# A decoder of four layers on one core: slots of two cross attentions interleaved with the closing steps around them, and a mixture's routing split by batches

## The reference

```python
x = x + L0_xattn(norm(x), ctx, ctx, mask)      # 16 heads of 8, additive mask
x = x + L0_ffn(norm(x))                        # mixture: 8 experts, top 2, one shared, GELU
x = x + L1_attn(norm(x))                       # "hyperbolic": softmax(-arccosh(q.k)^2 / sqrt(8))
x = x + L1_xattn(norm(x), ctx, ctx)            # 16 heads of 8
x = x + L1_ffn(norm(x))                        # mixture: 8 experts, top 2, one shared, SwiGLU

def L0_ffn(x):
    probs = softmax(x @ w_router.T)            # 8 logits for each token
    gates = one_hot_top2(probs) * values
    y = gelu(x @ W1 + b1) @ W2 + b2            # each expert, weighted by its gate
    return SCALE * (shared(x) + sum_e gates_e * y_e)
```

## Time and profile before

| what | us |
|---|---|
| median of 3 runs | 1261.74 (1260.95 to 1270.15) |
| the profiled execution, its own time | 1260.36 |
| its span, first to last instruction | 1259.0 |
| around the span | 1.4 |
| PE busy | 1029.4 (82%) |
| DVE busy | 803.8 (64%) |
| ACT busy | 609.9 (48%) |
| mean granted TensorE clock | 0.867 |

### The profile page before, as it was taken

One profiled execution on the slowest core, in us unless ns is written; L12 is line 12 of the kernel. 1 busy time (PEld: TensorE's weight loads), 2 busy tenths in 40 slices (PEclk: granted clock), 3 DMA queues, 4 the chain that ended last, 5 costly groups with the idle time before them and its releaser, 6 DMA issues.

```text
span 1259.0 us, 19879 instructions
## 1 busy us (share of the span) xinstructions
PE 1029.4 (82%) x7630; PEld 552.7 (44%) x7649; DVE 803.8 (64%) x2003; ACT 609.9 (48%) x1015; POOL 241.3 (19%) x305
## 2 busy tenths in 40 slices
PE   5777689998999974678585889999848978769999
PEld 4233223333577652344352233556513333336757
DVE  7786867722214467977856883487688877765412
ACT  2456345664333527768651778423115645423342
POOL 2923400000000223676441000000122000010000
PEclk9788879998899995757776899899956889989999
DMA  8332140000000210238012400800100300000000
GB/s 299 93 84 71 39 164 2 2 2 1 1 1 1 78 57 1 76 126 144 10 44 77 162 2 3 140 1 1 51 2 25 127 2 2 34 1 1 1 9 9
DMA packets 34785, 61.23 MB, mean 49 GB/s; under 512 B 4771, under 2 KB 25076, under 8 KB 33092
## 3 DMA queue, kind: packets, MB, share of 16 engines
q1 hardware_dynamic: 33828, 58.64, 16.6%
q10 hardware_dynamic: 864, 1.33, 0.3%
HBM read 42.91 MB, written 16.65 MB: 47 GB/s over the span
## 4 chain that ended last, share of the span: by engine, by line
PE 59%; DVE 28%; ACT 5%; issue 4%; DMA 2%; POOL 1%; SPq 0%; DVEq 0%; ACTq 0%; POOLq 0%
PE ps_s L869 9%; PE ps_e L859 9%; PE ps_v L662 6%; PE ps_e L598 5%; DVE mx L1816 5%; PE ps_s L619 3%; PE ps_e L596 3%; DVE ps_s L1812 2%; PE ps_s L943 2%; PE ps_e L956 2%; ACT work L1364 2%; DVE mx L1806 2%; DVE work L2290 2%; DVE work L2292 2%; DVE xn L1772 1%
## 5 line engine op out<-in xcount | busy, mean ns | idle before, releaser
L1364 ACT ACTIVATE work<-ps_e 128x512 f32<-128x512 f32 x448 | 250.8, 598 | 148.2 <-PE ps_e L598 143.0
L2557 POOL TENSOR_TENSOR rstd<-rstd,halves 128x2 f32<-128x2 f32 x52 | 36.6, 705 | 714.0 <-DVE rstd L1759 713.9
L1816 DVE TENSOR_REDUCE mx<-ps_s 128x2 f32<-128x1024 f32 x128 | 153.8, 1221 | 28.6 <-PE ps_s L619 27.1
L619 PE MATMUL ps_s<-ctx_stack,q_stack 49*128 49x512 bf16 (+1 forms) x384 | 130.2, 459 | 45.4 <-DVE mx L1816 32.9
L598 PE MATMUL ps_e<-q_stack,ctx_stack 52*128 52x256 bf16 (+1 forms) x768 | 151.2, 295 | 19.0 <-issue 6.5
L1466 ACT ACTIVATE work<-ps_s,keep 128x512 f32<-128x512 f32 x136 | 93.0, 687 | 144.8 <-PE ps_s L869 141.9
L662 PE MATMUL ps_v<-work,vaug 128*32 128x256 f32 x1536 | 131.9, 420 | 4.6 <-ACT work L1352 4.6
L859 PEld LDWEIGHTS ps_e<-ffn_w,work 128*128 128x128 f32 x960 | 119.1, 198 | 21.1 <-issue 19.9
L869 PE MATMUL ps_s<-xnT,ffn_w 128*128 128x512 f32 x240 | 119.2, 624 | 3.6 <-ACT work L1466 3.6
L859 PE MATMUL ps_e<-ffn_w,work 128*128 128x128 f32 x960 | 120.9, 281 | 0.8 <-DVE x L2006 0.8
L2016 DVE SCALAR_TENSOR_TENSOR x<-ps_e,gates,x 128x128 f32<-128x128 f32 x128 | 38.9, 346 | 126.5 <-PE ps_e L859 123.5
(11 more groups left out here) (375 smaller groups left out, 1800.7 us busy)
## 6 DMA issues: line engine op xcount, KB each, us to landing
q_stack<-q_scr SPq DMA_DIRECT2D x32, 192.0 KB
ffn_w<-in_L0f_w SPq DMA_DIRECT2D x1, 4608.0 KB, 14.7
ffn_w<-in_L1f_w SPq DMA_DIRECT2D x1, 3456.0 KB, 13.1
q_scr<-parts SPq DMA_DIRECT2D x16, 192.0 KB, 2.1
c_scr<-ffn_w SPq DMA_DIRECT2D x12, 256.0 KB, 7.5
kx_scr<-ffn_w SPq DMA_DIRECT2D x12, 256.0 KB, 3.4
ctx_stack<-kx_scr SPq DMA_DIRECT2D x2, 1536.0 KB
ctx_stack<-c_scr SPq DMA_DIRECT2D x2, 1536.0 KB
```

The lines of the kernel that those rows point to most:

```text
L619: return pe.matmul(ps_s[i][:, parity, :], q_stack[p0:p0 + n_rows, b, pair, part * P:(part + 1) * P], ctx_stack[p0:p0 + n_rows, pair, b * S ...
L1364: act.activation(pt[:, parity, :, :].rearrange("p k q -> p (k q)"), bank[f"e{parity}"], ACT.Exp).then_inc(exped, 1)
L1816: m = dve.tensor_reduce(mx[:, b, :, pair, part], ps_s[i][:], AX, ALU.max, negate=True)
```

## The change

1. **X0's end.** The main loop stops before slot 86 (TAILX). `l0_mixture` runs slots 86 to 95 itself with window_tile, and puts the 12 ups and their GELUs before slots 87 to 93 (1, 1, 2, 2, 2, 2, 2). On ACT too, the GELUs of a slot stand before what the slot itself does.
2. **L0 routing in two parts.** Batches 0 and 1 are routed in bank m at slot 66 of X0 (ACT's exponential and DVE's route_rest at slot 67), batches 2 and 3 after slot 95 in ps_s1, with DVE's route_rest at unit 1. The first half's gates and bias stand before unit 0, the second half's before unit 3 (GATES1).
3. **L1 routing.** The first half moves from slot 86 of X1 to slot 66, from bank e0 to m.
4. **X1's slots 16 to 19** go between the closing steps of the L1 attention's last batch: 16 before turn_close, 17 before l1_project_out, 18 before turn_norm, 19 before project. On DVE, slots 16 and 17 stand before add_out, 18 before the normalise, 19 after it.

```diff
+CLOSE_X1 = 4
+TAILX = 86
+GELU_FIRST = [(u, j) for u in range(3) for j in range(FJ)]
+GELU_BEFORE = {87: 1, 88: 1, 89: 2, 90: 2, 91: 2, 92: 2, 93: 2}
+ROUTE0 = 66
+GATES1 = 3
...
         def l0_mixture():
             n_exp = NE + 1
-            route("L0f", kp("L0f_router"))
-            pe.wait_ge(d_w, 16)
-            claim("s0")
-            for u in range(3):
-                for j in range(FJ):
+            done = 0
+            for t in range(TAILX, LAST[X0]):
+                if t == min(GELU_BEFORE):
+                    pe.wait_ge(d_w, 16)
+                    claim("s0")
+                for u, j in GELU_FIRST[done:done + GELU_BEFORE.get(t, 0)]:
                     gelu_up("L0f", u, j)
-            for g in range(2):
-                turn_gates("L0f", NE + 1, g, ROUTE_AT["L0f"])
-                gated_bias("L0f", 0, NE + 1, g)
+                done += GELU_BEFORE.get(t, 0)
+                cross_slot(X0, t, kp("L0x_fcT"), "L0f", window_tile)
+            pe.wait_ge(d_b2, 48)
+            route("L0f", kp("L0f_router"), 1, (2, 3), "s1")
+            turn_gates("L0f", NE + 1, 0, ROUTE_AT["L0f"])
+            gated_bias("L0f", 0, NE + 1, 0)
             for u in range(2 * n_exp):
                 g, e = divmod(u, n_exp)
+                if u == GATES1:
+                    turn_gates("L0f", NE + 1, 1, ROUTE_AT["L0f"] + 1)
+                    gated_bias("L0f", 0, NE + 1, 1)
...
+            cross_slot(X1, EARLY_X1, kp("L1x_oT"), "L1f")
             turn_close(A1, B - 1)
+            cross_slot(X1, EARLY_X1 + 1, kp("L1x_oT"), "L1f")
             l1_project_out(B - 1)
+            cross_slot(X1, EARLY_X1 + 2, kp("L1x_oT"), "L1f")
             turn_norm(X1, B - 1)
+            cross_slot(X1, EARLY_X1 + 3, kp("L1x_oT"), "L1f")
             project(X1, B - 1, kp("L1x_qT"))
...
-        for t in range(OVERLAP + LAST[X0]):
+        for t in range(OVERLAP + TAILX):
...
+            if t == OVERLAP + ROUTE0:
+                route("L0f", kp("L0f_router"), 0, (0, 1), "m")
...
-        for t in range(EARLY_X1, TAIL1):
+        for t in range(EARLY_X1 + CLOSE_X1, TAIL1):
             cross_slot(X1, t, kp("L1x_oT"), "L1f")
+            if t == ROUTE0:
+                route("L1f", kp("L1f_router"), 0, (0, 1), "m")
```

The ACT and DVE programs change in step; DVE's main part:

```diff
             n_exp = NE + 1
-            route_first("L0f")
-            route_rest("L0f", None)
-            for g in range(2):
-                turn_gates("L0f", n_exp, g)
-                gated_bias("L0f", g)
+            for t in range(TAILX, LAST[X0]):
+                cross_slot(X0, t, "L0f", window_tile)
+            dve.wait_ge(d_keep, 16)
...
+            route_first("L0f", 1, slice(4, 8), ps_s[1][:, 0, :])
+            turn_gates("L0f", n_exp, 0)
+            gated_bias("L0f", 0)
             for u in range(2 * n_exp):
                 g, e = divmod(u, n_exp)
+                if u == 1:
+                    route_rest("L0f", None, 1, slice(4, 8))
+                if u == GATES1:
+                    turn_gates("L0f", n_exp, 1)
+                    gated_bias("L0f", 1)
...
+            cross_slot(X1, EARLY_X1, "L1f")
+            cross_slot(X1, EARLY_X1 + 1, "L1f")
             add_out(A1, B - 1, ps_e[0][:, 0:S])
             statistics(X1, B - 1)
+            cross_slot(X1, EARLY_X1 + 2, "L1f")
             normalised(X1, B - 1)
+            cross_slot(X1, EARLY_X1 + 3, "L1f")
```

More of the change, by code:

```diff
@@ L410, in build @@
     EXPERTS = {"L0f": NE + 1, "L1f": NE + 1, "L3f": NE}
-    ROUTE_AT = {"L0f": 1, "L1f": 2, "L3f": 4}
+    ROUTE_AT = {"L0f": 1, "L1f": 3, "L3f": 5}
     UPS, HIDS = {"L0f": up_ps, "L1f": up_ps, "L3f": up3_ps}, {"L0f": hidden, "L1f": hidden, "L3f": hidden3}
@@ L963, in swiglu_tail @@
             for t in range(TAIL1, LAST[X1]):
-                if t == TAIL1:
-                    route("L1f", kp("L1f_router"), 0, (0, 1))
                 for u, j in SWIGLU_FIRST[done:done + SWIGLU_BEFORE.get(t, 0)]:
@@ L1318, in tensor_program @@
                 turn_mask(MASK_AT.index(t))
-        pe.wait_ge(d_b2, 48)
+            if t == OVERLAP + ROUTE0:
+                route("L0f", kp("L0f_router"), 0, (0, 1), "m")
         l0_mixture()
@@ L1470, in l0_mixture @@
             n_exp = NE + 1
-            route("L0f")
-            for u in range(3):
-                for j in range(FJ):
+            done = 0
+            for t in range(TAILX, LAST[X0]):
+                for u, j in GELU_FIRST[done:done + GELU_BEFORE.get(t, 0)]:
+                    if u == 2 and j == 0:
+                        act.wait_ge(summed, SUM0[X0] + 64)
                     gelu("L0f", u, j)
+                done += GELU_BEFORE.get(t, 0)
+                cross_slot(X0, t, "L0f")
+            route("L0f", 1, slice(4, 8))
             for u in range(1, 2 * n_exp):
@@ L1517, in swiglu_tail @@
             for t in range(TAIL1, LAST[X1]):
-                if t == TAIL1 + 1:
-                    route("L1f", 0, slice(0, 4))
                 for u, j in SWIGLU_FIRST[done:done + SWIGLU_BEFORE.get(t, 0)]:
@@ L1721, in scalar_program @@
                 turn_mask(MASK_AT.index(t))
-        act.wait_ge(d_keep, 16)
+            if t == OVERLAP + ROUTE0 + 1:
+                act.wait_ge(d_keep, 16)
+                route("L0f", 0, slice(0, 4))
         l0_mixture()
         l1_attention()
-        for t in range(EARLY_X1, TAIL1):
+        for t in range(EARLY_X1 + CLOSE_X1, TAIL1):
             cross_slot(X1, t, "L1f")
+            if t == ROUTE0 + 1:
+                route("L1f", 0, slice(0, 4))
         swiglu_ffn()
@@ L2024, in l0_mixture @@
             n_exp = NE + 1
-            route_first("L0f")
-            route_rest("L0f", None)
-            for g in range(2):
-                turn_gates("L0f", n_exp, g)
-                gated_bias("L0f", g)
+            for t in range(TAILX, LAST[X0]):
+                cross_slot(X0, t, "L0f", window_tile)
+            dve.wait_ge(d_keep, 16)
+            dve.tensor_scalar(bq_scaled[:], kp("L1x_bq"), RSQRT8, None, ALU.mult)
+            dve.wait_ge(d_b2, 48)
+            dve.tensor_scalar(maskrow[:], masku8[:], -1.0, BIG, ALU.add, ALU.mult).then_inc(mask_row, 1)
+            route_first("L0f", 1, slice(4, 8), ps_s[1][:, 0, :])
+            turn_gates("L0f", n_exp, 0)
+            gated_bias("L0f", 0)
             for u in range(2 * n_exp):
                 g, e = divmod(u, n_exp)
+                if u == 1:
[3 more added lines that the diff above has]
+                    gated_bias("L0f", 1)
                 for k in range(2):
@@ L2092, in swiglu_tail @@
             for t in range(TAIL1, LAST[X1]):
[L2093 to L2096, removed]
                 for u, j in SWIGLU_FIRST[done:done + SWIGLU_BEFORE.get(t, 0)]:
@@ L2531, in vector_program @@
                 cross_slot(X0, t - OVERLAP, "L0f")
[L2532 to L2535, removed]
+            if t == OVERLAP + ROUTE0:
+                route_first("L0f", 0, slice(0, 4), bank["m"])
+            if t == OVERLAP + ROUTE0 + 1:
+                route_rest("L0f", None, 0, slice(0, 4))
         l0_mixture()
         l1_attention()
-        for t in range(EARLY_X1, TAIL1):
+        for t in range(EARLY_X1 + CLOSE_X1, TAIL1):
             cross_slot(X1, t, "L1f")
+            if t == ROUTE0:
+                route_first("L1f", 0, slice(0, 4), bank["m"])
+            if t == ROUTE0 + 1:
+                route_rest("L1f", 1e-20, 0, slice(0, 4))
         swiglu_ffn()
```

## The result

The changed kernel takes 1248.44 us (median of 4 runs, 1246.21 to 1249.89) beside 1261.35 for the kernel before (4 runs): ratio 0.9877, 95% interval 0.9843 to 0.9911. Two later sets of runs of it gave 0.9915 (0.9887 to 0.9943) and 0.9866 (0.9833 to 0.9899). By the three ratios the gain is 11 to 17 us; the first medians are 12.9 apart, and I had forecast 8.7. The first ratio lies just beyond the 1% that I had taken as the bound of "no change", the second just short of it.

The account below looks back on a forecast made before the run. PE was taken to bound the kernel (59% of the chain), so only time on PE or with PE standing still counted. A to D -3.1, E -4.8 and F -0.8 summed to -8.7 us, 1253 by the median; range 1246 to 1262.

Parts of the forecast that it names:

- B: X0's end with ups between the closing steps: first L0 down at 323.7 instead of 331.10, -7.4 us, A included.
- C: Second gate block inside L0's unit loop, before unit 3: PE's waits and the block's steps cost together +3.3 us.
- D: Clock at L0's gates: same fall at the first block; possible new one at the second, 0 to 3.4 us, taken as 1.0.
- A: First half of L0's routing at slot 66 of X0: +1.05 us on a PE without slack.
- E: L1 attention's closing with X1's slots 16 to 19: slot 20's exponentials at 686.1 instead of 690.94, -4.8 us.
- F: L1's first routing half moved to slot 66: 1.88 us at 1.2 GHz out, 1.05 in, -0.8 us.
- R1: Clock stays up in L0's gates and X1's end because ups feed PE: -15 us, 1246; chance 0.20.
- R2: Clock falls and stays at 1.2 GHz through X0's end, ups run slow: +5.2 us, 1265.6; chance 0.08.
- R3: L1 closing stays late: maximum rows' DMA queues, lands at 688, E worth 2.9 us less, 1256; chance 0.12.

Follow-up runs that it names:

- e5: The changed kernel run again, unchanged, with a second profiled execution: 1251.86 us beside 1264.14 for the kernel before, ratio 0.9915.
- e1: Kernel before plus the X0's end and L0 routing edits alone (changed kernel without parts 3 and 4): 1258.26 us beside 1264.16, ratio 0.996.
- e12: Changed kernel with L1's first routing half back at slot 86, run a second time: 1250.2 us beside 1264.76 for the kernel before, ratio 0.9888.
- e13: The changed kernel a third time, unchanged: 1247.96 us, ratio 0.9866 to the kernel before.
- e2: Kernel before plus slots 16 to 19 of X1 in the L1 attention's closing alone: 1253.27 us, ratio 0.9924 to the kernel before.
- e4: Changed kernel with only L1's first routing half put back to slot 86: 1248.81 us, ratio 0.9882 to the kernel before.
- e3: Kernel before plus L1's first routing half at slot 66 instead of slot 86, alone: 1264.83 us, ratio 0.9999 to the kernel before.
- e9: Kernel before plus four tiny matmuls that nobody reads, behind slot 34 of X1: 1261.84 us beside 1262.73, ratio 0.9991.
- e10: Kernel of e2 plus twenty-two matmuls that nobody reads, behind slot 34 of X1: 1260.45 us, ratio 0.9985 to the kernel before.
- e7: Changed kernel with L0's routing in one piece behind X0's end, both gate blocks before the first down, ups still interleaved: 1256.74 us, ratio 0.9946 to the kernel before.

## Why the prediction was right or wrong

**B and C, the first mixture.** Right in kind, 1 to 2 us too careful (2 to 3 with D). First down: -8.3 us in the first execution, -9.1 in e5, with A in it, where I had -7.4. The three waits of PE for ACT that I put at 1.5 us came out at 1.14, 1.14 and 1.05, since the GELU in their way starts at the up's end (302.70, the up ends 302.66) and not 0.27 behind it. A was 0.9 instead of 1.05. C's block cost 3.3 as worked out: last down's end near 340.8, next up 344.14.

**D, the clock at the gates.** The second block did not bring the clock down, so the 1.0 for it was not due. The fall at the first block came, 6.8 us long in the first execution (318.4 to 325.2) and only 3.4 in e1 and e5, which is the difference between -5.2 and -6.4. The first two downs so took 5.85 us (5.47 in e5) instead of the 6.31 that I had left unchanged. A to D came out at -5.2 to -6.4 instead of -3.1.

The table load for the second routing stands in the rows above: 1.28 us at 316.30, and the exponential at 317.60, right behind it and 0.20 after DVE's subtraction that it waits for (317.21 and 0.19). By the Trainium skill (page "ScalarE: Activation LUTs", section "What ACT_TABLE_LOAD costs") load and drain would be 2.66 together; no drain of that size is seen here, and the row was the right one to go by.

**E, the closing.** -5.7 from turn to exponentials instead of -4.8. I had the query projection 1.3 us late; it came 7.02 behind the turn instead of 6.43, so 0.6. DVE's last reduction starts beside the projection and delays nothing.

**F, L1's routing.** Predicted -0.8; with the clock whole on both sides it is +1.1 at slot 66 and -1.5 at X1's end, -0.4, and e12 against e13 cannot see it. The bound of the earlier trace rows, 1.88 us at the old place, was a price at 1.2 GHz; in the changed kernel the end of X1 no longer runs at 1.2 GHz.

**The step that failed** is the clock at X1's end, a term that the sum put at nothing. I kept the fall of the earlier trace rows in the forecast and gave its absence to R1, for the reason that ups keep PE fed. The fall went away with the closing: e2, with the old routing and no ups in X0's end, has none, and e1, with the ups but not the closing, has it. The likely reason is that the closing puts X1's slots in another position against the clock's changes. The term measures -4.0 us (e2, e4, e12), the largest single miss. That 8.7 and 4.0 add to nearly the 12.9 of the medians is partly chance, since A to D and E were too careful as well and other stretches give time back. With what the stretches measured the sum reads: first mixture -5.2 to -6.4 (I had -3.1), closing -6.1 (-4.8), routing -0.4 (-0.8), X1's clock -4.0 (0), together -15.7 to -16.9. By their ratios the three sets of the changed kernel and the two of e4's lie at -11 to -17. What of the difference is given back in the L1 attention (-0.3 to +2.6) and behind 885 us (+0.6 to +11.8) I can't say: both stretches scatter between executions of one kernel, and the two profiles of the kernel before are the shortest of all behind 885 us. That stays open.

**The rivals.** R1 had the right size (-15, 1246) and one right half, the clock at X1's end, for a reason that e1 and e2 don't bear out. Its other half, the clock whole in L0's gates, did not happen at the first block. R2 did not happen: the clock was whole through the ups and waits, from 303 to 318. The argument against it was misread: in the earlier trace rows the clock was back after some 4.4 us of ups (311.4 to 315.9), not 10. The Trainium skill's rule on it (page "TensorE: Matmul & The Clock Gate", section "A second HAM failure mode: psum-queue depth-cycling") would have had PE's short waits bring the level down; in this trace two waits of 1.14 us among ups did not. R3 did not happen: L604 at slot 20 was not released by the rows' DMA. Its price was wrong too: a landing at 688 instead of 686.1 costs 1.9 us, and 2.9 is what is left of the gain, so it stood for 1255 and not 1256.

That the closing keeps the clock up is shown by e2 and by a count: ten executions of seven kernels with slots in the closing have no fall at X1's end, four of five of the others (the kernel before twice, e1, e3) have one in X1, and e9 is the fifth. That it does so by position is argued from the positions above and from e9, not shown: the run meant to shift a closing kernel back (e10) missed.

## What to carry to other kernels

Before pricing an edit, list the stretches behind it in which the clock is at half, and ask whether they lie beside a real shortage of work on PE or among busy slots. The latter can come and go with an edit elsewhere, as if they hung on position: here the closing, 110 us ahead, removed one (4.0 us), and e3 brought one (2.9), and they belong in the range with a chance of their own. Filling a chain of single steps with other matmuls pays only if the next thing that PE needs is ready when the filler is used up; here the ups brought nothing in the kernel whose routing was in one piece (e7). And free the first consumer of a DMA by placing its producer early: two of the four slots brought 3.7 of the closing's 6.1 us.

## What I had not expected of the hardware

With PE busy 3.10 of the 4 us before, the granted clock fell from 1.00 to 0.50 for 10.2 us in the kernel before (790.3 to 800.5 and, in its second execution, 788.2 to 798.4) and, with PE busy 3.77 of 4, in e3 (772.6 to 782.9); it did not in e9 with the same work, some 0.15 us later behind the clock's return. And in executions of one kernel (the changed one) the first 180 us differ by 4.6 us, after which the traces run parallel to 0.1 us for 100 to 180 us at a time (184 to 303 and 712 to 880 in the kernel before's time), and part again where the clock takes another course and in the L1 attention.
